# Window attention on one Trainium2 core: totals turned at step 38 with the reciprocal behind the maximum, and difference scores issued two steps ahead

## The chip, the core and the metric

The kernel runs on one core of a Trainium2 chip. The time is the device time of one execution in microseconds; the kernel before takes 2144.83 us, the median of three runs. TensorE, VectorE, ScalarE, GpSimd and the DMA queues each follow their own list of instructions and meet only at semaphores.

## What is computed

A post-norm transformer block over 8 sequences of 1024 rows with 256 columns: a windowed attention with 16 heads of 16 columns, a layer norm, then a second attention whose queries, keys and values come from tree-routed leaf networks, and another layer norm. The change touches the first attention only:

```python
q, k, v = split_heads(x @ Wq), split_heads(x @ Wk), split_heads(x @ Wv)
scores = jnp.einsum('bhqd,bhkd->bhqk', q, k) / math.sqrt(dh)
scores = jnp.exp(scores - jnp.max(scores, axis=-1, keepdims=True))
mask = (d <= half - 1) & (d >= -half)            # d = key - query, half = 32
scores = jnp.where(mask, scores, 0.0)
weights = jax.nn.softmax(scores, axis=-1)
out = jnp.einsum('bhqk,bhkd->bhqd', weights, v)
```

The maximum is over all 1024 keys, but only a window of 64 keys gets exp(score); all others count with the value 0 in the softmax that follows.

## The kernel before

**Units and steps.** The attention stage is 16 units, one for each sequence b and group g of 8 heads (u = 2b+g). A unit has 64 steps; step s handles head h = s // 8 and query tile q = s % 8, that is 128 queries against all 1024 keys. Each engine has the same loop over units and steps and does in each step its share of work of several ages: `late(b, g, s, LAG)` yields head hh in step 8 hh + LAG (running over into the next unit), so that work which comes once a head always falls on the same step modulo 8.

**The row maximum.** max(a, b) = b + relu(a - b), so each step needs two score products: the *difference scores* against d_stack (keys of the first half minus those of the second), into p_diff (2 banks, L1032), and the *half scores* against k_stack, into p_half (3 banks, L1036). ScalarE takes the Relu of p_diff into above (a ring of 4, L1156). VectorE adds p_half and takes the row maximum in one instruction (L1477). The waits: a difference product for step k waits until the Relu of step k-2 has emptied its bank, a half product for step k until the maximum of step k-3 is done, the Relu of step k for the maximum of k-4. In step s TensorE issues the difference product of s+1, then the half product of s+1.

**The window.** For each head, TensorE multiplies the window scores in two halves into one bank p_win, in the steps with lags 29 and 31 (L1049 to L1057; s % 8 = 5 and 7); the second half waits until ScalarE's first exponential has emptied the bank. ScalarE's two first exponentials (L1177) have lags 30 and 32, the second one over both halves (L1185) lag 33. In ScalarE's steps the Relu comes first, then the copy of row maxima, then a job's copy, then the exponentials.

**Weighted values, totals, turn.** At lag 35 TensorE multiplies weights and values into p_pv (L1076). At lag 36 VectorE reads the column outside the windows (`outside_values`, L1522) at the start of its step and adds it to the sums (`totals`, L1531) near the end of the step. At lag 39 TensorE turns the totals with two transposes (`turn`, L1087), VectorE takes the reciprocal of the denominators (`inverse`, L1539), at the very start of its step ahead of the maximum, and multiplies (`attention`, L1547) at the end of the step. `turn` waits for the totals, `inverse` for the turn.

**Jobs.** Beside this TensorE has two jobs every 8 steps (projections q, k of the next unit, values V, the output projection O, transposes T, X, R, sums S, ranks K), each in two parts in steps s % 8 = 0, 1 and 4, 5; ScalarE and VectorE handle their results at s % 8 = 2 and 6. The q, k and difference parts are copied by GpSimd, and SP loads them into the stacks for the next unit, six transfers a head; TensorE waits for the stack of head h ahead of its first difference product.

**Order in TensorE's step:** difference and half scores, transposed maxima, routing scores, jobs, window scores, turn, weighted values. Each engine works its list strictly in this written order.

Of the kernel before, what the change touches and what calls it, by code (L numbers as in the profile page):

```python
# [21 lines left out]
GH = 8  # L22
# [4 lines left out]
STEPS = GH * QT  # L27
# [44 lines left out]

WIN_LAGS = (29, 31)
EXP_LAGS, EXP2_LAG = (30, 32), 33
PV_LAG, TOTAL_LAG, TURN_LAG, ATT_LAG = 35, 36, 39, 39
VALUES_AT = (24, 45)
GROUPS, GROUP_ROWS = 4, 32
GROUP_BLOCKS = NBLK // GROUPS
# [57 lines left out]
def wait(eng, sem, value):  # L136

    if isinstance(value, int) and value <= 0:
        return
    eng.wait_ge(sem, value)  # L140


def alone(eng):

    eng.nop(nofuse=True)
# [66 lines left out]
def window_attention(nc, x, w_q, w_k, w_v, w_o, nets, x1, keep):  # L212
    with ExitStack() as ctx:
# [6 lines left out]
        def sem(name):  # L220
            return ctx.enter_context(nc.semaphore(name))
# [124 lines left out]
        s_diff = sem("diff_scores")  # L346
# [159 lines left out]
        def late(b, g, step, lag):  # L506

            for age in (1, 0):
                w = 2 * b + g - age
                for h in range(GH):  # L510
                    if 0 <= w < 2 * B and QT * h + lag == step + STEPS * age:
                        yield w, w % 2, h
# [323 lines left out]
        def _(pe):  # L836
# [77 lines left out]
            def unit(b, g):  # L914
                cur = 0 <= b < B
                u = 2 * b + g
                if g == 1 and b == -1:
                    pe.wait_ge(s_wlo, 4)
                    pe.wait_ge(s_whi, 4)
                    pe.wait_ge(s_const, CONSTANTS)  # L920
                if u == 0:
                    pe.wait_ge(s_nz, 5)
                    pe.wait_ge(s_small, 16 * 2 * NETS)
                    for c in (0, 1):
                        ins = nc.tensor.transpose(p_raw[:, 48 * c:48 * c + 48], node_raw[:, P * c:P * c + P],
                                                  ident[0:48, 0:48])
                    ins.then_inc(s_nt, 1)
                    pe.wait_ge(s_nlo, 1)
                for s in range(STEPS):
                    if cur:  # L930

                        if s == 0:
                            scores(u, g, 0, s_diff)
                        if s + 1 < STEPS:
                            scores(u, g, s + 1, s_diff)
                        if s == 0:
                            scores(u, g, 0, s_half)
                        if s + 1 < STEPS:
                            scores(u, g, s + 1, s_half)
                    for w, i, k in maxima(b, g, s, 0):  # L940
                        max_transpose(w, i, k)
                    for r, i, k in nodes(b, g, s, 0):
                        node_scores(r, i, k)
                    for part in (0, 1, 2):
                        for j, kind, i in jobs(b, g, s, part):
                            if kind != "d" and (part < 2 or kind == "S"):
                                job(b, g, j, kind, i, part)
                    for half in (0, 1):
                        for w, o, hh in late(b, g, s, WIN_LAGS[half]):
                            window_scores(w, o, hh, half)  # L950
                    for w, o, hh in late(b, g, s, TURN_LAG):
                        turn(GH * w + hh)
                    for w, o, hh in late(b, g, s, PV_LAG):
                        weighted_values(w, o, hh)
# [69 lines left out]
            def scores(u, g, s, which):  # L1024
                h, q = s // QT, s % QT
                k = STEPS * u + s
                qs = q_stack[0:SPLIT_ROWS, h, P * q:P * q + P]
                if which is s_diff:
                    if q == 0:
                        pe.wait_ge(s_stack[h], STACK_INC * (u + 1))  # L1030
                    wait(pe, s_above, k + 1 - reuse(s, 2))
                    nc.tensor.matmul(p_diff[s % 2][:], qs, d_stack[0:SPLIT_ROWS, h, :],  # L1032
                                     start=True, stop=True).then_inc(s_diff, 1)
                else:
                    wait(pe, s_max, k + 1 - reuse(s, 3))
                    nc.tensor.matmul(p_half[s % 3][:], qs,  # L1036
                                     k_stack[0:SPLIT_ROWS, h, HALO + S // 2:HALO + S],
                                     start=True, stop=True).then_inc(s_half, 1)
# [163 lines left out]
        def _(dve):  # L1202
# [256 lines left out]
            def unit(b, g):  # L1459
                cur = 0 <= b < B  # L1460
                u = 2 * b + g
                if u == 0:
                    nodes_low()
                    number_pages()
                for s in range(STEPS):
                    h, q = s // QT, s % QT
                    for w, o, hh in late(b, g, s, ATT_LAG):
                        inverse(GH * w + hh)
                    for w, o, hh in late(b, g, s, TOTAL_LAG):
                        outside_values(w, o, hh)  # L1470
                    if cur:

                        k = STEPS * u + s
                        dve.wait_ge(s_above, k + 1)
                        dve.wait_ge(s_half, k + 1)
                        alone(dve)
                        nc.vector.tensor_tensor_reduce(  # L1477
                            out=above[:, s % 4], in0=p_half[s % 3][:], in1=above[:, s % 4], scale=1.0, scalar=-3.0e38,
                            op0=ALU.add, op1=ALU.max, accum_out=row_max[g][:, s:s + 1]).then_inc(s_max, 1)
                    if g == 1 and 1 <= b < B and NORM_FIRST <= s < NORM_FIRST + QT:  # L1480
                        normalise(b - 1, s - NORM_FIRST)
                    for w, i, k in maxima(b, g, s, 1):
                        dve.wait_ge(s_mhi, k + 1)
                        wait(dve, s_mparts, k)
                        nc.vector.scalar_tensor_tensor(m_rest[:], p_max, -1.0, m_parts[:, 0, :],  # L1485
                                                       ALU.mult, ALU.subtract).then_inc(s_mrest, 1)
                    for j, kind, i in jobs(b, g, s, 2):
                        if kind not in "VS":
                            job(b, g, j, kind, i)
                    for j, kind, i in jobs(b, g, s, 3):  # L1490
                        if kind == "S":
                            job(b, g, j, kind, i)
                    for n in (0, 1):
                        for j, kind, i in jobs(b, g, s, STATS_LAGS[n]):
                            if kind == "O":
                                row_stats(b, g, j, 2 * i + n)
                    for j, kind, i in jobs(b, g, s, STATS_LAGS[2]):
                        if kind == "O":
                            row_mean_var(b, 2 * i)
                            row_mean_var(b, 2 * i + 1)  # L1500
                    for r, i, k in nodes(b, g, s, 1):
                        decide(r, i, k)
                    if g == 0 and 2 <= b < B and TREE_AT <= s < TREE_AT + TREE - 1:
                        tree(b - 2, s - TREE_AT)
                    if g == 0 and b == B and s == LAST_TREE:
                        for k in range(TREE - 1):
                            tree(b - 2, k)
                    for r, k in placing(b, g, s):
                        place(r, k)
                    for w, o, hh in late(b, g, s, TOTAL_LAG):  # L1510
                        totals(w, o, hh)
                    for w, o, hh in late(b, g, s, ATT_LAG):
                        attention(w, hh)

# [11 lines left out]
            def totals(w, o, h):  # L1526

                k = GH * w + h
                dve.wait_ge(s_base, k + 1)
                wait(dve, s_turn, k - 1)  # L1530
                nc.vector.tensor_tensor(total[:, k % 2].rearrange("p (c j) -> p c j", j=WIN), p_values[:, :, 0:WIN],  # L1531
                                        fixed[:, k % 2].unsqueeze(2).to_broadcast([P, GROUP_BLOCKS, WIN]),
                                        ALU.add).then_inc(s_tot, 1)

            def inverse(k):

                dve.wait_ge(s_turn, k + 1)
                wait(dve, s_att, k)
                nc.vector.reciprocal(inv[:], p_turn[:, :, :, TURN_AT + DH]).then_inc(s_inv, 1)  # L1539
# [659 lines left out]
```

## Time and profile before

| | |
|---|---|
| median of 3 runs | 2144.83 us (2141.4 to 2146.59) |
| the profiled execution | 2150.88 us, span 2148.9 us |
| TensorE / VectorE / ScalarE / GpSimd busy | 1845.2 / 1615.9 / 1333.1 / 897.3 us |
| attention stage | about 49 to 1258 us |
| score products, each kind | 1024 |
| mean granted TensorE clock | 0.94 of 2.4 GHz |

A row of the profile names the engine, the line of the kernel, the operation, and the tiles as out<-in. A row of the view in order of time begins with start and duration in us; merged instructions end in x and their count; brackets at the end give the idle time of the engine just before and who ended it. Ends of TensorE's products are modelled and overlap the next product. PEld is TensorE's load of weights, which can run ahead of its products; a wait can show there.

### The profile page before, as it was taken

Reading aid. Unit: us, or ns where it says so; the run is one execution under the profiler, and the core shown is the slowest. Engines: PE = TensorE matmul, PEld = TensorE weight load, DVE = VectorE, ACT = ScalarE, POOL = GpSimd, SP = SyncE. Lnnn points to the kernel's source line nnn. Section 1 sums busy time; section 2 is a strip of 40 time slices with the busy share of each in tenths; the row PEclk is TensorE's granted clock in tenths of the full one; section 3 lists DMA queues with packets and bytes.
Section 4 is the critical chain, followed back from the end, with each engine's and each line's share of the span. In section 5 each row is a group of like instructions: output and inputs, shape, how many; then the busy total and the mean of one; then the engine's idle time right before and its main releaser. Section 6 shows DMA issues by size and latency. Waiting matters only on the chain. (4 is left out here: it accounts for less than half of the span.)

```text
span 2148.9 us, 49579 instructions
## 1 busy us (share of the span) xinstructions
PE 1845.2 (86%) x16400; PEld 1352.9 (63%) x16400; DVE 1615.9 (75%) x4394; ACT 1333.1 (62%) x2515; POOL 897.3 (42%) x1338
## 2 busy tenths in 40 slices
PE   3988899889899898998988862877889599999997
PEld 2545556556455565564565551777778489999997
DVE  2887897977987978978978843796978367777775
ACT  2887787777787777777877722575766244444442
POOL 4422332554455456455545565000030755555511
PEclk8999999999999999999999965999999799999999
DMA  6443436336435535444454363969776333333311
GB/s 213 110 115 95 147 93 171 97 126 180 112 120 167 151 95 163 140 119 148 127 157 110 110 173 117 308 223 311 249 260 223 102 90 97 94 94 96 94 40 37
DMA packets 207318, 304.84 MB, mean 142 GB/s; under 512 B 48430, under 2 KB 108891, under 8 KB 207067
## 3 DMA queue, kind: packets, MB, share of 16 engines
q1 hardware_dynamic: 157322, 195.73, 31.1%
q0 software_dynamic: 29440, 68.98, 11.2%
q10 hardware_dynamic: 20304, 36.97, 4.7%
q8 instruction: 134, 2.20, 0.5%
q14 instruction: 118, 0.96, 0.2%
HBM read 104.16 MB, written 115.87 MB: 102 GB/s over the span
## 5 line engine op out<-in xcount | busy, mean ns | idle before, releaser
L1477 DVE CUSTOM_DVE_ANT_0 above<-p_half,above 128x512 f32<-128x512 f32 x1024 | 684.7, 681 | 99.2 <-ACT above L1156 66.9
L1156 ACT ACTIVATE above<-p_diff 128x512 f32<-128x512 f32 x1024 | 597.7, 605 | 224.1 <-PE p_diff L1032 213.3
L1036 PE MATMUL p_half<-k_stack,q_stack 96*128 96x512 bf16 x1024 | 402.9, 396 | 43.1 <-DVE row_max L1477 39.9
L1032 PE MATMUL p_diff<-d_stack,q_stack 96*128 96x512 bf16 x1024 | 406.3, 399 | 37.2 <-DMA d_stack<-d_parts 33.8
L1797 POOL DMA_INDIRECT raw<-sorted_y,slot x192 | 202.6, 1055 | 351.0 <-DMA sorted_y<-y_tile 295.9
L208 POOL DMA_INDIRECT sorted_x<-y,slot x192 | 198.6, 1034 | 92.7 <-issue 52.9
L2044 ACT ACTIVATE pt_hi<-p_one 128x512 fp32r<-128x512 f32 x128 | 69.5, 595 | 246.2 <-PE p_one L1920 246.2
L1036 PEld LDWEIGHTS p_half<-k_stack,q_stack 96*128 96x128 bf16 x1024 | 102.6, 101 | 139.7 <-DVE row_max L1477 117.7
L1177 ACT ACTIVATE w_win<-p_win 128x512 f32<-128x512 f32 x256 | 155.3, 607 | 47.7 <-PE p_win L1057 45.5
L1032 PEld LDWEIGHTS p_diff<-d_stack,q_stack 96*128 96x128 bf16 x1024 | 100.9, 99 | 127.3 <-issue 36.0
L1832 PE MATMUL p_out<-val_hi,pt_hi 128*128 128x256 f32 x512 | 151.8, 296 | 8.6 <-DVE val_lo L2113 7.9
L1832 PE MATMUL p_out<-val_hi,pt_lo 128*128 128x256 f32 x512 | 146.2, 286 | 0.0
L1832 PE MATMUL p_out<-val_lo,pt_hi 128*128 128x256 f32 x512 | 146.1, 285 | 0.0
L1185 ACT ACTIVATE w_win<-w_win 128x1024 f32<-128x1024 f32 x128 | 138.8, 1084 | 0.1
L776 POOL CAST m_parts<-m_rest 16x128 bf16<-16x128 f32 x64 | 18.1, 283 | 284.7 <-DVE m_rest L1485 284.6
L2100 DVE TENSOR_TENSOR y_tile<-p_pair,b 128x512 f32<-128x512 f32 x141 | 97.6, 692 | 37.0 <-DMA sorted_y<-y_tile 20.0
L2142 DVE TENSOR_REDUCE top<-p_pair 128x1 f32<-128x1024 f32 x64 | 78.3, 1224 | 56.5 <-PE p_pair L1832 55.8
L785 POOL DMA_DIRECT2D q_stack<-m_parts x192 | 99.7, 526 | 38.7 <-POOL m_parts L778 35.4
L1049 PE MATMUL p_win<-outside,ident_b 128*128 128x512 bf16 x256 | 101.6, 397 | 13.8 <-ACT w_win L1177 13.3
L1832 PE MATMUL p_pair<-tile_t_hi,w_tile 128*64 128x256 f32 x564 | 107.6, 284 | 0.0
L1076 PEld LDWEIGHTS p_pv<-w_win,v_win 128*32 128x32 f32 x4096 | 70.0, 117 | 57.6 <-issue 52.0
L2082 DVE TENSOR_TENSOR tile_t_lo<-p_one,tile_t_hi 128x512 fp32r<-128x512 f32 x141 | 96.3, 683 | 12.2 <-ACT tile_t_hi L1973 11.6
(281 smaller groups left out, 4985.4 us busy)
## 6 DMA issues: line engine op xcount, KB each, us to landing
sorted_x<-zeros SPq DMA_DIRECT2D x141, 256.0 KB, 3.1
x_tile<-sorted_x SPq DMA_DIRECT2D x141, 256.0 KB, 4.1
sorted_y<-y_tile ACTq DMA_DIRECT2D x141, 256.0 KB, 3.6
q_stack<-q_parts SPq DMA_DIRECT2D x256, 96.0 KB, 2.4
k_stack<-k_parts SPq DMA_DIRECT2D x256, 96.0 KB, 2.4
d_stack<-d_parts SPq DMA_DIRECT2D x256, 48.0 KB, 2.0
v_win<-v_tiles POOLq DMA_DIRECT2D x16, 544.0 KB, 5.2
v_win<-v_tiles POOLq DMA_DIRECT2D x32, 272.0 KB, 6.0
```

Source lines behind the costliest of these rows:

```text
L208: pool.indirect_dma_start(self.xs[n][:, :], bass.IndirectOffsetOnAxis(ap=where, axis=0), self.y[:, b % 2, t, :], None, bounds_check=IN_ROW ...
L785: pool.dma_start(q_stack[row:row + 1, 2 * i:2 * i + 2, :], m_parts[:, part, :]).then_inc(s_mrow, 16)
L1032: nc.tensor.matmul(p_diff[s % 2][:], qs, d_stack[0:SPLIT_ROWS, h, :], start=True, stop=True).then_inc(s_diff, 1)
L1036: nc.tensor.matmul(p_half[s % 3][:], qs, k_stack[0:SPLIT_ROWS, h, HALO + S // 2:HALO + S], start=True, stop=True).then_inc(s_half, 1)
L1049: nc.tensor.matmul(p_win[:].rearrange("p (i j) -> p i j", j=WIN), ident_b[:], outside[:].unsqueeze(1).to_broadcast([P, NBLK // 2, WIN]), s ...
L1156: nc.scalar.activation(above[:, s % 4], p_diff[s % 2][:], ACT.Relu).then_inc(s_above, 1)
L1177: nc.scalar.activation(w_win[:, h % 2, NBLK // 2 * half:NBLK // 2 * half + NBLK // 2, 0:WIN], p_win[:].rearrange("p (i j) -> p i j", j=WIN ...
L1185: nc.scalar.activation(weights, weights, ACT.Exp).then_inc(s_ww, 1)
L1477: nc.vector.tensor_tensor_reduce(out=above[:, s % 4], in0=p_half[s % 3][:], in1=above[:, s % 4], scale=1.0, scalar=-3.0e38, op0=ALU.add, o ...
L1797: pool.indirect_dma_start(raw[b % 2][:, n, t, :], None, ys[n][:, :], bass.IndirectOffsetOnAxis(ap=where, axis=0), bounds_check=OUT_ROWS - ...
L1832: ins = nc.tensor.matmul(out_, l, r, start=first and n == 0, stop=last and n == 2)
L2100: nc.vector.tensor_tensor(yo[:, j % 3], p_y[j % 2].rearrange("p (t c) -> p t c", t=2), b2[n % 2][:, bass.ds(leaf * C, C)].unsqueeze(1).to_ ...
```

## The change

The totals are turned at lag 38 instead of 39. VectorE does its totals right behind the maximum of the same step, and the reciprocal (still lag 39) behind the maximum instead of in front of it. TensorE issues in step s the difference product of step s+2 instead of s+1; at the start of a unit it issues those of 0 and 1, then the half product of 0. Half products stay one step ahead. Banks, rings and semaphores are as before.

```diff
-PV_LAG, TOTAL_LAG, TURN_LAG, ATT_LAG = 35, 36, 39, 39
+PV_LAG, TOTAL_LAG, TURN_LAG, ATT_LAG = 35, 36, 38, 39
 ...
                         if s == 0:
                             scores(u, g, 0, s_diff)
-                        if s + 1 < STEPS:
-                            scores(u, g, s + 1, s_diff)
-                        if s == 0:
+                            scores(u, g, 1, s_diff)
                             scores(u, g, 0, s_half)
+                        if s + 2 < STEPS:
+                            scores(u, g, s + 2, s_diff)
                         if s + 1 < STEPS:
                             scores(u, g, s + 1, s_half)
 ...
                     h, q = s // QT, s % QT
-                    for w, o, hh in late(b, g, s, ATT_LAG):
-                        inverse(GH * w + hh)
                     for w, o, hh in late(b, g, s, TOTAL_LAG):
                         outside_values(w, o, hh)
 ...
                             op0=ALU.add, op1=ALU.max, accum_out=row_max[g][:, s:s + 1]).then_inc(s_max, 1)
+                    for w, o, hh in late(b, g, s, TOTAL_LAG):
+                        totals(w, o, hh)
+                    for w, o, hh in late(b, g, s, ATT_LAG):
+                        inverse(GH * w + hh)
 ...
                         place(r, k)
-                    for w, o, hh in late(b, g, s, TOTAL_LAG):
-                        totals(w, o, hh)
                     for w, o, hh in late(b, g, s, ATT_LAG):
                         attention(w, hh)
```

## Rows read from the trace of the kernel before

**Rows 1.** The row of VectorE's score reduction (L1477), by line: durations min/median/max, first and last start

```profile
L1477 DVE CUSTOM_DVE_ANT_0 above<-p_half,above x1024: 625/682/694, 49.0 to 1235.7; 128x512 f32<-128x512 f32 x171
```

**Rows 2.** Busy us by stretch: PE, PEld, DVE, ACT, POOL; granted clock, DMA share, GB/s

```profile
200.00:1183.00 983.00, 889.74 (x9084) 545.37 (x9083) 818.85 (x2638) 747.71 (x1381) 476.89 (x753) 0.96 0.47 135
1183.00:1258.00 75.00, 60.70 (x695) 35.98 (x694) 53.98 (x179) 47.22 (x84) 40.04 (x65) 0.82 0.29 86
```

**Rows 3.** TensorE in order of time, 646 to 655 us: start, us, instruction

```profile
646.60 0.40 PE L1057 MATMUL p_win<-q_stack,k_stack 99*128 99x64 bf16 x8
646.83 0.38 PE L1032 MATMUL p_diff<-d_stack,q_stack 96*128 96x512 bf16 x1
647.05 0.38 PE L1036 MATMUL p_half<-k_stack,q_stack 96*128 96x512 bf16 x1
...
647.74 0.39 PE L1049 MATMUL p_win<-outside,ident_b 128*128 128x512 bf16 x1
...
648.00 0.40 PE L1057 MATMUL p_win<-q_stack,k_stack 99*128 99x64 bf16 x8
648.23 0.39 PE L1087 MATMUL p_pv<-ident,total 113*128 113x113 f32 x2
...
651.31 0.38 PE L1032 MATMUL p_diff<-d_stack,q_stack 96*128 96x512 bf16 x1
...
654.27 0.40 PE L1057 MATMUL p_win<-q_stack,k_stack 99*128 99x64 bf16 x8
```

**Rows 4.** Who waited for whom, 48 to 1258 us: total us, times, longest

```profile
ACT above L1156 <- PE p_diff L1032: 213.3, 264, 10.6
...
PEld p_half L1036 <- DVE row_max L1477: 117.7, 197, 3.6
DVE above L1477 <- ACT above L1156: 66.9, 146, 1.5
DVE inv L1539 <- PE p_pv L1087: 63.3, 82, 2.5
...
PEld p_win L1049 <- ACT w_win L1177: 44.8, 86, 2.4
...
PEld p_diff L1032 <- ACT above L1156: 31.2, 100, 1.1
...
PEld p_diff L1032 <- DMA d_stack<-d_parts: 23.0, 8, 4.5
```

**Rows 5.** ScalarE in order of time, the same stretch

```profile
647.09 0.60 ACT L1177 ACTIVATE w_win<-p_win 128x512 f32<-128x512 f32 x1
647.56 1.11 ACT L1156 ACTIVATE above<-p_diff 128x512 f32<-128x512 f32 x2
648.52 0.64 ACT L1177 ACTIVATE w_win<-p_win 128x512 f32<-128x512 f32 x1
...
651.45 0.61 ACT L1156 ACTIVATE above<-p_diff 128x512 f32<-128x512 f32 x1
```

**Rows 6.** VectorE in order of time, the same stretch

```profile
648.66 0.21 DVE L1539 RECIPROCAL inv<-p_pv 128x8 f32<-128x8 f32 x1 [0.48 <-PE p_pv L1087]
...
651.25 0.69 DVE L1477 CUSTOM_DVE_ANT_0 above<-p_half,above 128x512 f32<-128x512 f32 x1 [0.32 <-ACT above L1156]
```

**Rows 7.** TensorE and ScalarE in order of time, first of the 98 heads

```profile
143.63 0.40 PE L1057 MATMUL p_win<-q_stack,k_stack 99*128 99x64 bf16 x8
...
148.28 0.38 PE L1032 MATMUL p_diff<-d_stack,q_stack 96*128 96x512 bf16 x1
...
150.97 0.40 PE L1057 MATMUL p_win<-q_stack,k_stack 99*128 99x64 bf16 x8
...
148.47 0.60 ACT L1156 ACTIVATE above<-p_diff 128x512 f32<-128x512 f32 x1
```

**Rows 8.** TensorE in order of time, last of the 98 heads

```profile
1186.51 0.40 PE L1057 MATMUL p_win<-q_stack,k_stack 99*128 99x64 bf16 x8
...
1195.69 0.40 PE L1057 MATMUL p_win<-q_stack,k_stack 99*128 99x64 bf16 x8
```

## Prediction

> **What bounds the kernel now.** I read the granted clock and the busy time by stretch first, then who waits for whom, then one eight-step stretch in order of time, because the change only reorders waits inside the attention stage. That stage runs from the first row maximum at 49.0 us to the last at 1235.7 us [rows 1], so 1186.7 us for 16 units of 64 steps, 9.27 us for each eight steps (one head). No engine fills it: in its middle VectorE is busy 818.9 of 983 us, ScalarE 747.7, and TensorE's 889.7 overstates it [rows 2], since a score product is listed with 0.38 us while the next one starts 0.22 us later (646.83, 647.05) [rows 3]. The time is set by a chain that changes engines, and the question is which waits close it. The list of waits [rows 4] shows ScalarE waiting 213.3 us for difference scores, VectorE waiting 66.9 us for ScalarE's result and 63.3 us for the turned totals ahead of the reciprocal, and TensorE's weight loads held 117.7 us by the maxima and 44.8 us by the first exponential. The change goes after the first three.
>
> In order of time [rows 3, 5] one loop is tight. With r for the step modulo 8: TensorE makes the first half of the window products at r=5 (ends 647.00). ScalarE's first exponential starts 0.09 us later, at 647.09, and ends at 647.69. TensorE's second half (r=7) starts at 647.74, 0.05 us after that. ScalarE meanwhile does the Relu steps of r=7 and r=0 (647.56, two of them, to 648.67), the second exponential half (648.52), a Relu, the long exponential and the Relu of r=2, nearly back to back.
>
> **The change part by part.**
>
> *Difference scores two steps ahead.* No product is added. But p_diff has two banks, so the product for step s+2 must wait until ScalarE has emptied step s. At its step s TensorE now waits for Relu(s); before, it waited for Relu(s-1). Behind the waiting product stand, in TensorE's order, the half scores of s+1, the jobs, the window products, the turn and the weighted values of that step; ScalarE's exponentials and VectorE's maxima wait for those.
>
> At r=7 this bites. ScalarE's order is first exponential (its step r=6), then Relu(r=7). So TensorE, which before put the second window half right behind the first exponential, must now wait for the Relu after it. In the head of [rows 3, 5]: the exponential ends 647.69; the first of the two Relus started 647.56 and takes 0.6 (as the single one at 651.45 does), so it ends about 648.18; with 0.05 for the semaphore the difference product starts 648.23, half scores 648.45, window products 648.67 instead of 647.74. Their results are there 0.66 us later (647.74 to 648.40 before), so ScalarE's second half can start at 649.37 instead of 648.52: 0.85 us in which ScalarE has nothing that its order lets it do. The long exponential and Relu(r=2), Relu(r=3) come 0.85 us later too.
>
> At r=2 and r=3 TensorE must then wait for exactly those. Before, its step r=3 began at 651.31, ahead of the end of Relu(r=3) at 652.06 (started 651.45, 0.61) [rows 3, 5], and its two jobs and the weighted values went on beside ScalarE's burst. Now weighted values, both job parts and the next window half (r=3 to 5) start only behind Relu(r=3). The eight steps become a serial loop of two phases:
> - ScalarE's phase, first window half's results to Relu(r=3): 647.00 to 652.06 = 5.06 us, plus the 0.85 = 5.91;
> - TensorE's phase, head of step r=3 to the next window half's results: 651.31 to 654.67 = 3.36 us.
> With 0.05 between them 9.32 us, where the trace has 654.67 - 647.00 = 7.67. The first head of the stage's second unit gives, by the same steps [rows 7], 144.03 to 149.07 = 5.04, plus 0.85, plus 148.28 to 151.37 = 3.09: 9.03, against 7.34.
>
> I did this for all 98 heads of the 14 middle units whose loop lies inside one unit (the first is that of [rows 7], the last that of [rows 8], with 5.69, 0.14 and 4.41: 10.29 against 9.18). Means: ScalarE's phase 5.44, its delay 0.76, TensorE's phase 3.85, so 10.10 us, against 9.08 in the trace: +1.02 us a head. That is the upper end: in both phases it keeps stalls that belong to the old chain (TensorE held by the maxima, the inverse's wait). The lower end: TensorE reaches r=7 on average 1.03 us ahead of the end of the Relu that it now needs (the same heads, worked out in the same way); up to 0.39 of it is used by the turn that moves in front, and the stalls that it has today at the half scores (117.7 us as the weight loads show them [rows 4], 0.9 a head) can swallow most of what is left: +0.1 us. I take +0.75, nearer the upper end, because the walked heads show no TensorE stall at all that could swallow the wait.
>
> *What it gives back.* ScalarE's 213.3 us of waits for difference scores [rows 4] fall, but VectorE gains only where ScalarE was late for lack of them: the burst r=6 to r=2 is late because of its own work, as the waits of the maxima at 651.25 (0.32 us) [rows 6] stand right behind the Relu. Counted at nothing beyond what the loop already has.
>
> *Totals turned at step 38, reciprocal behind the maximum.* The turn is two transposes, listed with 0.39 us (648.23) [rows 3]. At r=6 it is hidden by the new wait at r=7; without that cover it costs what it did before, since nothing is added. Its own wait, for the totals of r=4, is met: totals now stand right behind the maximum of r=4, TensorE's half scores at r=6 wait for that same maximum, and a total takes 0.42 us; bounds 0 and 0.2 us a head, taken 0. The reciprocal's 63.3 us of waiting go (648.66 had waited 0.48 [rows 6]): the turn is over before the half scores of that step can be reduced. What is late next for VectorE is Relu(r=7), ending 648.18 here, so its maximum moves from 648.81 to about 648.35. But the maximum of r=2 (651.25) waited for ScalarE in any case [rows 6] and now waits 0.85 more. Gain at the end of the loop: 0, bounds 0 and 0.5 us a head.
>
> *Unit boundaries.* At step 0 the product for step 2 waits for Relu(0) ahead of the half scores of 1: up to 0.6 us, on 16 units. There TensorE already waits for the stacks to land (23.0 us, 8 times [rows 4]), whose loads hang on the last eight steps' jobs; a later arrival only shortens that wait. The later stacks are asked for one step earlier too (step 6 for 7); no wait for them shows beyond those 8, and with slower heads they have more room: 0. I count the 7 heads inside each of 16 units, 112, and nothing for the rest. SP's and GpSimd's queues keep their order.
>
> **Sum.** 112 x 0.75 = 84 us. The profiled execution took 2150.9 us (span 2148.9), 6.1 above the median of 2144.8; the rest of the kernel follows the stage in order and moves with it. 2144.8 + 84 = 2229 us.
>
> **Rivals.**
> - *VectorE is the bound and the waits simply go.* It is the busiest engine, and its 63.3 and 66.9 us of waits [rows 4] are what the change aims at. If TensorE came to r=7 after Relu(r=7) anyway, half of them (65 us) would be the gain: 2080 to 2125, middle 2110. Against it: window half and exponential stand 0.05 us apart. Chance 0.10.
> - *It is swallowed.* TensorE's stalls at half scores and the reciprocal's gain cover the new wait (the lower end, 0.1 us a head and below): 2138 to 2160. Chance 0.10.
> - *The turn waits for the totals and nothing else changes* (the change doesn't do what it says): within 5 us of 2145. Chance 0.03.
> - *The clock falls.* From 1183 to 1258 us, where TensorE has least to do, the granted clock is 0.82, against 0.96 in 200 to 1183 us [rows 2]. With more waits the whole stage might go there: of each loop some 5 us are TensorE's, times 0.96/0.82 - 1 = 0.17, is 0.85 us, x 112 = 95 us on top: up to 2324. I give 0.10 to a time above 2285. The Trainium skill, "TensorE: Matmul & The Clock Gate", Part 1, puts it as a rule: throttled is the default state and activity releases it, with 1.2 and 2.4 GHz as the only two levels. By that rule this rival would be the likely one; the trace agrees on the direction only, since the middle keeps 0.96 with all its present waits.
>
> **Chances and range.** Forecast (2165 to 2285, with 0.5 and 1.2 us a head as its ends) 0.67; clock 0.10; swallowed or nothing 0.13; faster 0.10. About 0.3% (6 us) is what a measurement can tell from no change. Faster 0.11, same 0.06, slower 0.83. Range 8 in 10: 2155 to 2290.
>
> **What would show it.** Right: TensorE's waits for the Relu (difference product released by ScalarE's L1156) rise from 31.2 us [rows 4] to over 100, with the largest at r=7; ScalarE gains waits for the second window half; the reciprocal waits for nothing; waits of the half scores for the maxima fall; the loop from window half to window half is about 9.9 us. Wrong: if the window half at r=7 still starts within 0.1 us of the first exponential's end, or if the heads keep 9.1 us, the serial loop was no loop, and the time stays at or below 2145.

## The result and the profile after

The changed kernel takes 2246.57 us (median of 4 runs, 2241.04 to 2257.51) against 2145.71 for the kernel before in the same comparison: ratio 1.0487, 95% interval 1.0455 to 1.052. The forecast was slower, 2229 us, with 2155 to 2290 as the range. The span grew from 2148.9 to 2239.1 us, 90.2 us.

All of it, and a little more, lies in the attention stage. The row that answers to [rows 1] (the score reduction of VectorE; durations, then first and last start) gives 1328.0 - 47.5 = 1280.5 us, where the kernel before had 1186.7: 93.8 us more.

```profile
L1475 DVE CUSTOM_DVE_ANT_0 above<-p_half,above x1024: 646/685/694, 47.5 to 1328.0; 128x512 f32<-128x512 f32 x171
```

Busy time by stretch, with the columns of [rows 2]: the first line is the middle of the stage, the second its end. The granted clock is 0.97 and 0.81 where [rows 2] had 0.96 and 0.82, so the clock took nothing. VectorE and ScalarE do the same work in a longer time.

```profile
200.00:1280.00 1080.00, 930.15 (x9352) 557.60 (x9355) 855.79 (x2710) 768.67 (x1421) 487.66 (x770) 0.97 0.43 126
1275.00:1350.00 75.00, 56.85 (x636) 34.66 (x633) 47.59 (x156) 42.65 (x74) 35.05 (x58) 0.81 0.25 77
```

Who waited for whom in the stage (48 to 1350 us; total, times, longest), answering to [rows 4]:

```profile
PEld p_diff L1032 <- ACT above L1156: 306.6, 448, 2.2
DVE above L1475 <- ACT above L1156: 174.2, 270, 2.1
...
ACT w_win L1177 <- PE p_win L1057: 145.6, 164, 4.3
ACT above L1156 <- PE p_diff L1032: 130.9, 162, 4.8
...
PEld p_half L1036 <- DVE row_max L1475: 16.3, 37, 1.4
...
PEld p_diff L1032 <- DMA d_stack<-d_parts: 7.2, 6, 2.3
```

Against [rows 4]: the waits that the change aims at did shrink (the difference scores that ScalarE waits for from 213.3 to 130.9; of the reciprocal's 63.3 us, 1.5 are left). What replaced them is larger: TensorE is held by the Relu for 306.6 us instead of 31.2, ScalarE by the window products for 145.6 instead of 45.5, and VectorE by the Relu for 174.2 instead of 66.9. TensorE's waits for the maxima (117.7 before, 16.3 now) nearly vanish: TensorE now mostly comes to its half product after the maximum that would have held it.

The list of the kernel before (48 to 1258 us) has this line for the window products:

```profile
ACT w_win L1177 <- PE p_win L1057: 45.5, 63, 4.1
```

Split by the step in which TensorE issues the waiting product, the 306.6 us of the first line are about 94 at step 7 of eight, 63 at step 1, 70 at step 2, 61 at step 3, and little elsewhere.

The head of [rows 3, 5], the same one of the same unit, in order of time (start, duration), TensorE first:

```profile
697.56 0.40 PE L1057 MATMUL p_win<-q_stack,k_stack 99*128 99x64 bf16 x8
697.79 0.38 PE L1032 MATMUL p_diff<-d_stack,q_stack 96*128 96x512 bf16 x1
698.01 0.38 PE L1036 MATMUL p_half<-k_stack,q_stack 96*128 96x512 bf16 x1
698.23 0.36 PE L1087 MATMUL p_pv<-ident,total 113*128 113x113 f32 x2
699.14 0.39 PE L1032 MATMUL p_diff<-d_stack,q_stack 96*128 96x512 bf16 x1 [0.56 <-ACT above L1156]
699.37 0.38 PE L1036 MATMUL p_half<-k_stack,q_stack 96*128 96x512 bf16 x1
699.59 0.38 PE L1049 MATMUL p_win<-outside,ident_b 128*128 128x512 bf16 x1
...
703.89 0.39 PE L1032 MATMUL p_diff<-d_stack,q_stack 96*128 96x512 bf16 x1 [0.34 <-ACT above L1156]
...
706.87 0.40 PE L1057 MATMUL p_win<-q_stack,k_stack 99*128 99x64 bf16 x8
```

```profile
698.01 0.59 ACT L1177 ACTIVATE w_win<-p_win 128x512 f32<-128x512 f32 x1
698.49 1.09 ACT L1156 ACTIVATE above<-p_diff 128x512 f32<-128x512 f32 x2
700.27 0.60 ACT L1177 ACTIVATE w_win<-p_win 128x512 f32<-128x512 f32 x1 [0.69 <-PE p_win L1057]
...
703.25 0.59 ACT L1156 ACTIVATE above<-p_diff 128x512 f32<-128x512 f32 x1
```

The first exponential ends at 698.60. The difference product of step 7 of eight is released by the Relu only at 699.14, the window half starts at 699.59, 0.99 us behind the exponential where [rows 3, 5] had 0.05, and ScalarE stands idle for 0.69 us before its second half. The Relu of step 3 ends at 703.84, and the product that waits for it starts at 703.89. So the loop from window half to window half takes 707.27 - 697.96 = 9.31 us: 5.88 for ScalarE's phase, 0.05, and 3.38 for TensorE's. The working of the prediction gave 5.91, 0.05, 3.36 and 9.32 for this head, so it is right here to 0.03 us. It is not so in every head, as the part on the prediction shows.

VectorE in the same head shows that it got what the change meant to give it, and where it lost it again. The reciprocal follows its maximum with no wait (0.48 us in [rows 6]); the maxima of steps 1 and 2 then wait 0.51 and 0.73 us for the Relu.

```profile
699.26 0.69 DVE L1475 CUSTOM_DVE_ANT_0 above<-p_half,above 128x512 f32<-128x512 f32 x1
699.87 0.08 DVE L1475 DVE_READ_ACCUMULATOR2_ANT row_max<- 128x1 f32 x1
699.87 0.20 DVE L1539 RECIPROCAL inv<-p_pv 128x8 f32<-128x8 f32 x1
...
701.52 0.69 DVE L1475 CUSTOM_DVE_ANT_0 above<-p_half,above 128x512 f32<-128x512 f32 x1 [0.51 <-ACT above L1156]
...
702.95 0.69 DVE L1475 CUSTOM_DVE_ANT_0 above<-p_half,above 128x512 f32<-128x512 f32 x1 [0.73 <-ACT above L1156]
```

Over the same 98 heads the means are: loop 9.08 us before and 10.04 after; from the end of the first exponential to the start of its second half 0.94 and 1.68; from the same end to the second window half 0.18 and 0.99.

### The profile page after: what moved, and what is told of

It is laid out like the page before. It is cut to its first block and busy times, and to the rows that moved or that the text cites. A ratio compares the mean times of both kernels' runs of the same rounds, so it can differ in the third digit from the quotient of the medians.

```text
span 2239.1 us, 49579 instructions
## 1 busy us (share of the span) xinstructions
PE 1866.3 (83%) x16400; PEld 1351.7 (60%) x16400; DVE 1633.5 (73%) x4394; ACT 1333.0 (60%) x2515; POOL 896.3 (40%) x1338
## 5 line engine op out<-in xcount | busy, mean ns | idle before, releaser
L1475 DVE CUSTOM_DVE_ANT_0 above<-p_half,above 128x512 f32<-128x512 f32 x1024 | 691.9, 683 | 197.9 <-ACT above L1156 174.2
L1156 ACT ACTIVATE above<-p_diff 128x512 f32<-128x512 f32 x1024 | 581.2, 598 | 144.7 <-PE p_diff L1032 141.5
L1177 ACT ACTIVATE w_win<-p_win 128x512 f32<-128x512 f32 x256 | 152.8, 597 | 147.1 <-PE p_win L1057 145.6
L1036 PEld LDWEIGHTS p_half<-k_stack,q_stack 96*128 96x128 bf16 x1024 | 103.1, 101 | 26.0 <-DVE row_max L1475 16.3
L1057 PE MATMUL p_win<-q_stack,k_stack 99*128 99x64 bf16 x2048 | 105.1, 195 | 0.0
L1832 PEld LDWEIGHTS p_out<-val_hi,pt_hi 128*128 128x128 f32 x512 | 99.6, 194 | 8.9 <-issue 8.9
```

The costliest lines, as they stand in the source:

```text
L1036: nc.tensor.matmul(p_half[s % 3][:], qs, k_stack[0:SPLIT_ROWS, h, HALO + S // 2:HALO + S], start=True, stop=True).then_inc(s_half, 1)
L1057: ins = nc.tensor.matmul(p_win[:, WIN * n:WIN * n + WIN], k_stack[0:ROWS, h, WIN * i:WIN * i + P], q_stack[0:ROWS, h, WIN * i:WIN * i + WI ...
L1156: nc.scalar.activation(above[:, s % 4], p_diff[s % 2][:], ACT.Relu).then_inc(s_above, 1)
L1177: nc.scalar.activation(w_win[:, h % 2, NBLK // 2 * half:NBLK // 2 * half + NBLK // 2, 0:WIN], p_win[:].rearrange("p (i j) -> p i j", j=WIN ...
L1475: nc.vector.tensor_tensor_reduce(out=above[:, s % 4], in0=p_half[s % 3][:], in1=above[:, s % 4], scale=1.0, scalar=-3.0e38, op0=ALU.add, o ...
L1832: ins = nc.tensor.matmul(out_, l, r, start=first and n == 0, stop=last and n == 2)
```

## The experiments

Twelve kernels ran, on more than one chip; on the chip of the first four the kernel before itself took 2215 us, so everything is compared as a ratio to the kernel before on the same chip, with its 95% interval. Two kernels that ran on different chips are compared through their ratios alone. An expectation in us is meant against 2145 us for the kernel before. Figures given by step or by head are sums and means worked out from the instructions in the traces, not rows of a view. The theory is the loop; its rivals are named in each expectation.

**Each part alone.** *diff_alone* is the kernel before with the difference products two steps ahead:

```diff
                             scores(u, g, 0, s_diff)
-                        if s + 1 < STEPS:
-                            scores(u, g, s + 1, s_diff)
-                        if s == 0:
+                            scores(u, g, 1, s_diff)
                             scores(u, g, 0, s_half)
+                        if s + 2 < STEPS:
+                            scores(u, g, s + 2, s_diff)
```

> The kernel before with one part of the change: difference products two steps ahead; turn at lag 39 and reciprocal ahead of the maximum as before. Loop theory (the difference product waits for the Relu of its own step and holds the second window half, so ScalarE idles between its two first exponentials): all of the loss is here, 2230 to 2270 us, the second exponential half starts about 1.7 us behind the end of the first one (0.94 before), and the reciprocal, whose turn now comes later, waits over 100 us in all. Rival (the moved totals and reciprocal cost the time on VectorE): within 10 us of 2145.

Measured: 1.0504 (1.0463 to 1.0545). Of the stage in its trace (its slower chip is in these sums), the reciprocal's waits rise from 63.3 to 165.4 us, as the turn now stands behind the late window half; ScalarE waits 132.0 us for window products.

```profile
PEld p_diff L1032 <- ACT above L1156: 309.3, 378, 4.1
DVE inv L1539 <- PE p_pv L1087: 165.4, 114, 4.0
```

*turn_alone* is the rest of the change without that part (lag 38, totals and reciprocal behind the maximum).

> The kernel before with the other part alone: turn at lag 38, totals and reciprocal behind the maximum, difference products one step ahead. Loop theory: the reciprocal's 63 us of waits go, the turn is out of the way behind the second window half; VectorE is held by the Relu of step 2 of eight in any case: 2115 to 2145 us. Rival (moved totals and reciprocal cost the time): 2200 us or more.

Measured: 0.9961 (0.994 to 0.9983), about 8 us of gain. The whole loss is in the difference products; the other part is a small gain.

**The price of the wait at step 7.** *wait_at_7* takes the kernel before, keeps every order, and adds one wait ahead of the second window half:

```diff
                 wait(pe, s_e1, 2 * k + half)
+                if half == 1:
+                    wait(pe, s_above, min(QT * k + WIN_LAGS[1] + 1, 2 * B * STEPS))
```

> The kernel before with one wait added and no order changed: the second window half waits for the Relu of its own step (s % 8 = 7), as the change makes it do. Loop theory: it starts 0.5 us later, ScalarE's second exponential half some 0.3 us later, for VectorE the turn comes 0.5 us later: ratio 1.01 to 1.03. Rival (the wait at step 7 has slack): ratio below 1.005.

Measured: 1.0231 (1.0184 to 1.0278). The one wait costs some 50 us, nearly half of the loss, without a single product moved. Not all of that need be ScalarE's hole: here the turn still stands behind the late window half, so the reciprocal waits 126.3 us in its trace (63.3 before), and in the changed kernel 1.5. ScalarE's waits for window products, 45.5 us before:

```profile
ACT w_win L1179 <- PE p_win L1059: 78.1, 153, 4.6
```

**Taking the early product out of one step after another.** *late_at_7* is the changed kernel, with the difference product of s+2 issued behind the window half when s % 8 = 7:

```diff
-                        if s + 2 < STEPS:
+                        if s + 2 < STEPS and s % 8 != 7:
                             scores(u, g, s + 2, s_diff)
 ...
+                    if cur and s % 8 == 7 and s + 2 < STEPS:
+                        scores(u, g, s + 2, s_diff)
                     for w, o, hh in late(b, g, s, PV_LAG):
                         weighted_values(w, o, hh)
```

> The changed kernel, but in the steps s % 8 = 7 the difference product of s+2 is issued behind the second window half and not at the head of the step. Loop theory: the hole of 0.74 us a head between ScalarE's two exponentials closes; with 112 to 120 heads 80 us come back: 2150 to 2180 us, the rest being the waits at steps 1 to 3 of eight. Rival (the waits at steps 1 to 3 are the cause by themselves, step 7 only comes first): 2220 us or more.

Measured: 1.0128 (1.0097 to 1.0159). From 1.0487 that is 3.6%, some 77 us back, and the hole between ScalarE's two exponentials is closed (0.92 us from end to start, 0.94 before). Step 7 is the largest part, but not all.

*late_at_7_to_2* treats the steps 7, 0, 1 and 2 so, and issues the product behind the weighted values:

> The changed kernel with the difference product of s+2 behind all other work of the step at s % 8 = 7, 0, 1 and 2, and at the head in the other four. Loop theory: the waits for ScalarE's burst hold nothing but the head of the next step, as in the kernel before: ratio 0.985 to 1.005. Rival (the remaining early products cost too): ratio 1.01 or more.

Measured: 1.0146 (1.0111 to 1.0182). The expectation failed. Nothing was gained over late_at_7, although TensorE's waits for the Relu fell from 199.3 to 122.1 us in all. The stall ahead of the product that is issued in step 3, behind which the weighted values stand, was there in late_at_7 and stayed as it was: 68.1 us of the weight loads' waits there, 69.0 here. The waits at steps 0 to 2, most of which did go, bought nothing while that one stood. So step 3 was taken out next, then 4 and 5.

*late_at_7_to_3* adds step 3:

> As late_at_7_to_2, with step 3 of eight among the late ones, so that weighted values no longer stand behind the wait for the Relu of step 3. Loop theory: the last 1.5% of loss are that wait (0.44 us a head at the product issued in step 3): ratio 0.985 to 1.003. Rival (something else in the early products costs): ratio stays above 1.01.

Measured: 1.0069 (1.0046 to 1.0092). Better by 0.8%, but above the interval expected, and below the rival's; 0.09 and 0.13 us a head were left ahead of the products issued in steps 4 and 5.

*late_at_7_to_5* adds steps 4 and 5, so that only step 6 is early:

> As late_at_7_to_3, with steps 4 and 5 of eight late too; only at step 6 the difference product is still early. Loop theory: the last 0.7% over before (1.1% over turn_alone) are the waits ahead of the job parts and the first window half in steps 4 and 5 (0.09 and 0.13 us a head in late_at_7_to_3): ratio 0.993 to 1.000, that of turn_alone. Rival (being ahead at the unit's start or at step 6 costs): ratio 1.004 or more.

Measured: 0.9979 (0.9961 to 0.9998): the loss is gone, and what stays is near the gain of turn_alone. TensorE's waits for the Relu fall along this row of kernels; here the line of the changed kernel, then of late_at_7, late_at_7_to_2, late_at_7_to_3 and late_at_7_to_5, each from its own list of waits:

```profile
PEld p_diff L1032 <- ACT above L1156: 306.6, 448, 2.2
```

```profile
PEld p_diff L1034 <- ACT above L1158: 199.3, 354, 1.5
```

```profile
PEld p_diff L1034 <- ACT above L1158: 122.1, 224, 1.1
```

```profile
PEld p_diff L1034 <- ACT above L1158: 92.2, 232, 1.1
```

```profile
PEld p_diff L1034 <- ACT above L1158: 51.3, 143, 1.0
```

**Half products first.** *half_first* is the changed kernel with the two products of a step exchanged, so that the half product of s+1 goes ahead of the one that waits.

> The changed kernel with the half product of s+1 ahead of the difference product of s+2 in every step. Loop theory: the half products go free but the window half still stands behind the waiting difference product: 2225 to 2255 us. Rival (VectorE is starved of half scores by the waiting product): the loss goes, 2140 to 2180 us.

Measured: 1.0283 (1.0251 to 1.0315), between the two theories and outside the interval of each. The means by head suggest why: the window half still starts 0.81 us behind the first exponential (0.99 after), and the stalls remain (214.6 us in the row of the weight loads), but a half product, 0.22 us from its start to the next one's, now runs inside each stall and not behind it. The loop holds several such stalls a head, and I had not counted that. This is an argument from the trace; no run takes it apart. That VectorE was starved of half scores is not supported: what it waited for in the changed kernel was the Relu (174.2 us), not the half scores (9.5 us).

**Taking the cause away.** *relu_ahead* leaves TensorE as the change has it and moves ScalarE's Relu one step ahead too, in front of the exponentials of the step:

```diff
                     if cur:
-                        k = STEPS * u + s
-                        act.wait_ge(s_diff, k + 1)
-                        wait(act, s_max, k - 3)
-                        nc.scalar.activation(above[:, s % 4], p_diff[s % 2][:], ACT.Relu).then_inc(s_above, 1)
+                        for r in (([0] if s == 0 else []) + [s + 1] if s + 1 < STEPS else []):
+                            k = STEPS * u + r
+                            act.wait_ge(s_diff, k + 1)
+                            wait(act, s_max, k - 3)
+                            nc.scalar.activation(above[:, r % 4], p_diff[r % 2][:], ACT.Relu).then_inc(s_above, 1)
```

> The changed kernel, and ScalarE takes the Relu one step ahead too (in its step s that of s+1, so in front of the exponentials, not behind them). Loop theory: the Relu that TensorE needs at step 7 is done before the first exponential, the hole and the serial loop go, and the time is within 1.5% of before, rather below: ratio 0.98 to 1.005. Rival (issuing the difference products early costs by itself, on TensorE or in the banks): ratio stays above 1.03.

Measured: 0.9947 (0.9926 to 0.9968), faster than both kernels. ScalarE in the same head as above: the Relu that TensorE's step 7 needs (642.54) is done ahead of the first exponential (643.51), the second half starts at 645.01, 0.90 us behind the first one's end at 644.11, and the burst runs on without a hole.

```profile
642.54 0.60 ACT L1157 ACTIVATE above<-p_diff 128x512 f32<-128x512 f32 x1
643.04 0.59 ACT L1121 ACTIVATE rt_hi<-p_job 128x512 fp32r<-128x512 f32 x1
643.51 0.60 ACT L1178 ACTIVATE w_win<-p_win 128x512 f32<-128x512 f32 x1
643.99 1.11 ACT L1157 ACTIVATE above<-p_diff 128x512 f32<-128x512 f32 x2
645.01 0.60 ACT L1178 ACTIVATE w_win<-p_win 128x512 f32<-128x512 f32 x1
```

*relu_ahead_diff1* moves the Relu ahead, but leaves the difference products one step ahead (with the turn's part of the change):

> ScalarE's Relu one step ahead, turn at 38 and reciprocal behind the maximum, but difference products one step ahead as before. Loop theory: the first exponential now stands behind a Relu whose product TensorE issues at the head of step 6, behind the first window half: ScalarE waits some 0.3 to 0.8 us more a head: ratio 1.00 to 1.05. Rival (order on ScalarE is all that matters): ratio below 0.995.

Measured: 1.0354 (1.0309 to 1.0399). The mirror image of the change: now ScalarE's first exponential stands behind a Relu whose product TensorE has not issued yet. ScalarE waits 313.4 us for difference scores, and TensorE's second window half waits for the exponential. Neither engine may run ahead alone.

```profile
ACT above L1157 <- PE p_diff L1032: 313.4, 432, 10.6
PEld p_win L1049 <- ACT w_win L1178: 136.5, 127, 2.0
```

*relu_ahead_turn39* has Relu and difference products ahead, but turn, totals and reciprocal as before:

> Difference products two steps ahead and ScalarE's Relu one step ahead, but turn at 39 and the reciprocal ahead of the maximum, totals at the end of the step, as in the kernel before. If the turn's part is worth something once ScalarE is no longer late at step 2 of eight: ratio 0.005 to 0.02 above that of relu_ahead (1.000 to 1.015). Rival (it is worth nothing, the reciprocal's wait is covered): within 0.003 of 0.995.

Measured: 1.0026 (1.0005 to 1.0047), 0.8% above relu_ahead. The turn's part looks worth twice as much here as alone (0.4%), but the two kernels ran on different chips and the intervals are wide enough to leave the factor open. The reciprocal waits 80.6 us in this trace. That VectorE keeps more of what the reciprocal gives back, because ScalarE is no longer late at step 2, would explain it and is not shown.

*relu_ahead_half_first* is relu_ahead with the half product first:

> relu_ahead with the half product of s+1 ahead of the difference product of s+2. Loop theory: little waits for the Relu any more, so the order of the two products moves less than 0.5%: ratio 0.990 to 1.000. Rival (half products are what VectorE is short of): below 0.990.

Measured: 0.991 (0.9884 to 0.9936), 2123.35 us, the fastest of all, about 0.4% under relu_ahead. The two intervals overlap and come from different chips, so that difference is not settled; nor is the rival's "below 0.990" shut out, for the interval reaches 0.9884. Against it: VectorE's waits for half scores are longer here (68.7 us) than in relu_ahead (25.6).

## Why the prediction was right, step by step

- *The place.* A product issued two steps ahead with two banks waits for the Relu of its own step, and at step 7 of eight that Relu stands behind the first exponential. Shown by the trace (0.69 us of idle ScalarE in the walked head), by wait_at_7, which pays 2.3% for that wait alone, and by late_at_7, which gets 3.6% back.
- *The delay of ScalarE.* 0.76 us a head were worked out; 1.68 - 0.94 = 0.74 were measured.
- *The signs named ahead.* All came: TensorE's waits for the Relu above 100 us (306.6), the largest of them at step 7 (about 94), the reciprocal's gone (1.5), and a loop near 9.9 us (10.04).
- *The serial loop.* 10.10 us a head was its full value and 10.04 was measured, but the agreement of the sums is in part luck. In the same 98 heads of the changed kernel ScalarE's phase is 5.80 us, where 5.44 + 0.76 = 6.20 were worked out, TensorE's is 3.70, where 3.85 were, and between the two lie 0.54 us on average and not 0.05. In 65 of the 98 heads TensorE's step 3 starts within 0.1 us of the end of the Relu, as the loop says. In the other 33 TensorE is later, held by something the loop leaves out. In one of them the Relu ends at 754.75 us, but the product that waited for it starts only at 756.20, because TensorE was held by VectorE's part of a ranking job:

```profile
754.95 0.44 PE L886 MATMUL p_job<-ident,x_in 128*128 128x128 f32 x2 [1.46 <-DVE rest L1287]
...
756.20 0.38 PE L1032 MATMUL p_diff<-d_stack,q_stack 96*128 96x512 bf16 x1
```

  So the old stalls that the upper end kept did shrink, by 0.55 us in the two phases, as the prediction warned; waits outside the loop, put at nothing, gave 0.49 of it back. The choice of +0.75 us between +0.1 and +1.02 was too low: measured is +0.96. At 112 heads this term is 107 us, not 84.
- *Unit boundaries at nothing.* The stage grew by 93.8 us, so the rest of it gave back 14 us. Over the whole stage the 111 loops inside a unit grew by 110 us together, and the 16 that cross a boundary shrank by 18. The later arrival shortens the wait for the stacks, from 23.0 to 7.2 us; the prediction said so and counted no gain. This error and the one before it pull in opposite directions. The median is off by 18 us; some 10 of these come from the executions compared, as the two profiled spans lie 90.2 us apart and the two medians 100.9.
- *The range.* Its lower end was said to be 0.5 us a head, but 112 x 0.5 us gives 2201 and not 2165. Nothing hangs on it here.
- *The turn at nothing.* In the changed kernel it could not be told apart (diff_alone and the change overlap). Alone it is 8 us of gain, which the bounds of 0 to 0.5 us a head allowed.
- *Difference scores one step earlier give nothing at the end of the loop.* Right as long as ScalarE's order stays; with ScalarE moved too they give a gain, together with the turn.
- *Rivals.* VectorE's waits were not simply taken away (its wait for the Relu rose to 174.2 us); the loss was not swallowed; the clock didn't move, although TensorE waited far more: 0.97 in the middle of the stage, near the higher of its two levels, 2.4 GHz. The Trainium skill, "TensorE: Matmul & The Clock Gate", Part 1, has throttled as the default state and activity as what releases it. The trace agrees in direction only: TensorE was busy in 930 of the 1080 us of the middle at 0.97, and in 57 of the last 75 us at 0.81. That a fall was therefore likely was the prediction's own inference, and it did not come.

What stays open: how much of the loss each of steps 4 and 5 holds (they were taken out together); why half_first gains just 2%, which was argued from the stalls and not measured apart; and what sets the loop in the 33 heads where TensorE is later than the Relu, of which only one was followed.

## What to carry to other kernels

Issuing a product n steps ahead into n banks makes the producer wait for the consumer's work of the same step; ask what stands ahead of that work in the consumer's list and what stands behind the waiting product in the producer's. If a pipeline is made deeper on one engine, make the consumer's list deeper by the same step: either engine ahead alone cost 3.5 to 5% here, both together gained 0.5%. Another bank might serve as well, but that was not tried. When a loop through two engines is found, check each of its phases afterwards and not only their sum, and test a suspected wait by adding it alone to the old kernel. A total of waits is no measure of time: taking 77 us of TensorE's waits away at steps 0 to 2 gained nothing while the one at step 3 stood.

## What was not expected of the hardware

Nothing in the durations: the same instructions took the same time before and after (a score reduction 682 and 685 ns, median). New to me was only how little the granted clock minded: TensorE's row of waits for the Relu grew tenfold at 0.96 and 0.97 of full speed.
